# Expert layer 1's last table part in two classes, and the first group of the delta layer loaded, normalised and turned inside the expert layer's block

## The reference, cut to what matters

```python
x = x + linear_attention(layernorm(x))      # 16 heads, relu random features
x = x + expert_ffn(layernorm(x))            # 8 experts, top 2 of a softmax router
x = x + fast_weight_memory(layernorm(x))    # "delta": sequence over the 8 batches, own layer norm at its end
x = x + expert_ffn(layernorm(x))            # the same expert weights again
```

## Time and profile before

| what | value |
|---|---|
| median of 3 runs | 1044.81 us |
| the 3 runs | 1044.81, 1048.1, 1034.82 us |
| the profiled execution's own time | 1036.21 us |
| its span, first to last instruction | 1034.4 us |
| mean granted TensorE clock | 0.976 of full speed |
| PE busy | 946.9 us, 92% of the span |
| DVE, ACT, POOL busy | 54%, 52%, 36% of the span |

### The profile page before, as it was taken

How to read it: one execution, slowest core, us unless ns; L and a number is a source line. 1 busy time by engine, 2 the same in 40 slices (tenths; PEclk the granted TensorE clock), 3 DMA queues, 4 the chain that set the end, 5 groups by cost and what they waited for, 6 DMA issues and landing times.

```text
span 1034.4 us, 31649 instructions
## 1 busy us (share of the span) xinstructions
PE 946.9 (92%) x11919; PEld 701.9 (68%) x11919; DVE 553.6 (54%) x1979; ACT 534.6 (52%) x1082; POOL 367.6 (36%) x387
## 2 busy tenths in 40 slices
PE   7999999999999889969998899999999898897885
PEld 6445665566689889965544674595467697887775
DVE  5236355534574511207688478868768756671014
ACT  3443434342325344536776766775775754455553
POOL 2200331232135555543140102134321637465554
PEclk9999999999999899989999999999999999799998
DMA  8734412441213223213020301020216222223236
GB/s 219 209 83 83 105 48 63 98 104 47 66 51 86 66 69 83 59 58 125 4 83 18 83 29 34 13 92 19 60 51 220 60 57 66 55 58 85 76 110 205
DMA packets 80308, 82.77 MB, mean 80 GB/s; under 512 B 12207, under 2 KB 63236, under 8 KB 79648
## 3 DMA queue, kind: packets, MB, share of 16 engines
q1 hardware_dynamic: 66512, 59.87, 22.3%
q0 software_dynamic: 10176, 19.04, 6.0%
q10 hardware_dynamic: 3472, 1.84, 0.8%
HBM read 53.96 MB, written 27.64 MB: 79 GB/s over the span
## 4 chain that ended last, share of the span: by engine, by line
PE 37%; DVE 7%; ACT 5%; issue 3%; another core or an unknown queue 2%; DMA 1%; POOL 0%; ACTq 0%; POOLq 0%; DVEq 0%; SPq 0%
PE b_ring L1917 8%; PE b_ring L1366 6%; PE b_ring L1859 5%; PE b_ring L1377 5%; PE b_g L1970 4%; PE b_g L1939 4%; PE b_ring L1987 3%; DVE b_kq L2347 2%; ACT early L2102 2%; ACT b_v L1392 1%; ACT b_outT L2114 1%; ACT b_kq L1401 1%; PE b_r L248 1%; DVE b_coef L2258 1%
## 5 line engine op out<-in xcount | busy, mean ns | idle before, releaser
L1917 PE MATMUL b_ring<-b_hT,b_qkT 128*128 128x512 f32 x256 | 120.7, 608 | 5.3 <-DVE b_kq L2347 4.4
L2347 DVE SCALAR_TENSOR_TENSOR b_kq<-b_exp,b_ring 128x512 f32<-128x512 f32 x128 | 83.1, 684 | 35.6 <-ACT b_exp L2080 33.8
L1366 PE MATMUL b_ring<-b_v,b_kq 128*128 128x128 f32 x568 | 79.9, 285 | 23.9 <-ACT b_v L1387 20.2
L278 POOL DMA_INDIRECT expert_rows<-f_route_sent,f_route_place_id x64 | 62.0, 969 | 103.5 <-DVE f_route_place_id L234 50.8
L1366 PEld LDWEIGHTS b_ring<-b_v,b_kq 128*128 128x128 f32 x568 | 71.3, 197 | 30.9 <-ACT b_v L1387 25.8
L2080 ACT ACTIVATE b_exp<-b_ring 128x512 f32<-128x512 f32 x128 | 73.6, 604 | 29.7 <-PE b_ring L1917 17.5
L1366 PE MATMUL a_ring<-phik 128*128 128x128 f32 x568 | 78.8, 283 | 9.9 <-ACT phik L1387 9.2
L1917 PEld LDWEIGHTS b_ring<-b_hT,b_qkT 128*128 128x128 f32 x256 | 45.3, 189 | 61.4 <-issue 39.4
L278 POOL DMA_INDIRECT expert_rows<-g_route_sent,g_route_place_id x48 | 53.3, 1110 | 87.9 <-PE b_ring L1987 33.5
L1039 ACT ACTIVATE phik<-a_ring 128x512 f32<-128x512 f32 x64 | 38.2, 597 | 81.4 <-PE a_ring L882 79.1
L1366 PEld LDWEIGHTS a_ring<-phik 128*128 128x128 f32 x568 | 71.4, 197 | 12.6 <-ACT phik L1387 10.5
(11 more groups left out here) (344 smaller groups left out, 1854.6 us busy)
## 6 DMA issues: line engine op xcount, KB each, us to landing
a_rn_wide<-norm_compact SPq DMA_DIRECT2D x28, 512.0 KB, 10.0
wide<-in_L_ffn_W SPq DMA_DIRECT2D x32, 256.0 KB, 6.5
a_rn_wide<-expert_rows SPq DMA_DIRECT2D x71, 65.0 KB
b_coef<-gram_compact SPq DMA_DIRECT2D x4, 1024.0 KB, 4.9
b_hT<-expert_rows SPq DMA_DIRECT2D x56, 65.0 KB
x<-in_L_attn_a_x SPq DMA_DIRECT2D x8, 256.0 KB, 4.2
early<-expert_parts SPq DMA_DIRECT2D x4, 512.0 KB
gram_compact<-wide SPq DMA_DIRECT2D x32, 64.0 KB
```

The source lines that it names most:

```text
L278: pool.indirect_dma_start(self.rows, bass.IndirectOffsetOnAxis(self.place_id[:, k, n:n + 1], 0), self.sent[:, n, k, :], None).then_inc(sel ...
L1366: ins = pe.matmul(self.hid_bank[j % 2][:, f * P:(f + 1) * P], self.w1_now[:, b % W1_SLOTS, f * P:(f + 1) * P], self.blkT[:, b % HID_SLOTS, ...
L1917: pe.matmul(ring[n % 4][:, :], w, hT[:, g % 2, half * 512:half * 512 + 512], start=True, stop=True)\
L2347: dve.scalar_tensor_tensor(out=kq[:, p % 2, half:half + FOURS // 2, slot:slot + T * FOUR], in0=exps[:, n % EXPS, :].rearrange("p (a n) -> ...
```

## The change

1. The second table part is made in two classes of rows: first all rows that were routed up to the first of the last batch's four tiles, then the rest. `marked` is the router's count at that point. `A_NEXT` = 65: all rows of group 0 lie in blocks 0 to 64. The number of blocks stays 71.
2. SP loads group 0 when the blocks below `A_NEXT` are stored (with pairs, blocks 0 to 65), all four DMAs on SP, into `early`. It waits for the rest of the scatters behind the load. ACT loads nothing.
3. Five of the nine weight fills are turned beside blocks j = 22, 24, 26, 28 and 30, the other four behind the last block, in the two banks `a_y` and `a_t`.
4. DVE's additions, statistics and normalisation of group 0, POOL's roots, PE's turn and ACT's copy stand at the end of the first block (`FirstGroup`). The ones in `hT` are set by DVE at j = 30.
5. The block ends with `no_gpsimd_drain=True`.
6. `mix`, `own` and the router's start stand between the `kq` steps 15, 23 and 27 of group 0. SP loads groups 1, 2 and 3 without a wait.
7. `h` and `hT` and one buffer of the attention share a new tile `late`.

```diff
+A_NEXT = (2 * (TOKENS - (SEQ - P)) + EXPERTS * (P - 1)) // P
...
         block_table = BlockTable(K, C, "f", rows, rn_flat[...][:, 0:1280], ((0, A_FULL), (A_FULL, BLOCKS)),
+                                 {1: 1}, router.before[:, 1, :])
-        block = ctx.enter_context(nc.Block())
+        turn_banks, TURNED_BESIDE, TURN_AT = (y_bank, t_bank), 5, 22
+        block = ctx.enter_context(nc.Block(no_gpsimd_drain=True))
...
                 ffn.fetch(sp, j)
-            load_first_part(sp, K, C, ffn, parts, 0)
+            memory_weights.rows_turned(sp, K, TURNED_BESIDE)
+            ffn.stored_before(sp, A_NEXT)
+            first_group.load(sp)
+            ffn.stored(sp)
...
+                elif j in range(TURN_AT, TURN_AT + 2 * TURNED_BESIDE, 2):
+                    memory_weights.turn(pe, (j - TURN_AT) // 2, turn_banks)
+            for n in range(TURNED_BESIDE, memory_weights.FILLS):
+                memory_weights.turn(pe, n, turn_banks)
+            for half in range(2):
+                first_group.turn(pe, half, wide_bank[half])
...
-            load_first_part(act, K, C, ffn, parts, 1)
+                elif j in range(TURN_AT, TURN_AT + 2 * TURNED_BESIDE, 2):
+                    memory_weights.read(act, (j - TURN_AT) // 2, turn_banks)
+            for n in range(TURNED_BESIDE, memory_weights.FILLS):
+                memory_weights.read(act, n, turn_banks)
+            act.wait_ge(C["brows_less"], 15)
+            for half in range(2):
+                first_group.turned(act, half, wide_bank[half])
...
                 ffn.scatter(pool, j)
+            for half in range(2):
+                first_group.root(pool, half)
...
+                elif j == 30:
+                    first_group.ones(dve)
+            for half in range(2):
+                first_group.add(dve, half)
+            for half in range(2):
+                first_group.normalize(dve, half)
...
-            weights.turn(pe, weight_banks)
-            pe.wait_ge(weights.bank_read, weights.read0 + weights.FILLS)
-            turn(0)
             keys_and_queries(0)
...
+                    if g == 0 and n == 15:
+                        dve.memset(mix[:, :, :, :], 0.0)
+                    if g == 0 and n == 23:
+                        own_block()
+                    if g == 0 and n == 27:
+                        router.begin(dve)
```

More of the change, by code:

```diff
@@ L393, in count @@
             dve.tensor_copy(self.C["tail"][:, :], self.C["filled"][:, :]).then_inc(self.tail_ready, 1)
-        self.rows_of(dve, self.n_blocks, last)
-        if phase + 1 in self.marks:
+        if last and self.marked is not None:
+            self.rows_of(dve, self.touched[:, 0, :], True, self.marked)
+        self.rows_of(dve, self.n_blocks, last, self.C["filled"][:, :])
+        if phase + 1 in self.marks and self.marked is None:
             self.mark(dve, self.marks[phase + 1] - 1)
@@ L683, in less_last, with turn @@
         store_less_last(dve, C["beta_rows"][:, :, :], (C["brows_less"], 12), 0.0)
-    def turn(self, pe, banks):
+    def turn(self, pe, n, banks):
         C, ident = self.C, self.C["ident"]
[L690 to L703, removed]
@@ L721, in linear_attention @@
-def linear_attention(K, C, A, inp, normd, rows, parts):
+        b = banks[n % len(banks)]
+        if n >= len(banks):
+            pe.wait_ge(self.bank_read, self.read0 + n - len(banks) + 1)
+        if n < 6:
+            for j in range(4):
+                ins = pe.transpose(b[:, j * P:(j + 1) * P], C["b_rows"][:, 4 * n + j, :], ident[:, :])
+        elif n == 6:
+            ins = pe.transpose(b[:, 0:HEADS], C["beta_rows"][:, 0, :], ident[0:HEADS, 0:HEADS])
+        else:
+            for j in range(4):
+                q = 4 * (n - 7) + j
+                ins = pe.transpose(b[:, j * P:(j + 1) * P], C["wo_rows"][:, q * P:(q + 1) * P], ident[:, :])
@@ new lines, in turn, with read @@
+        ins.then_inc(self.bank_full, 1)
+    def read(self, act, n, banks):
+        C = self.C
+        b = banks[n % len(banks)]
+        act.wait_ge(self.bank_full, self.full0 + n + 1)
+        if n < 6:
+            dst, o = (C["b_qkT"], n) if n < 4 else (C["b_vT"], n - 4)
+            ins = act.copy(dst[:, o * 512:o * 512 + 512], b[:, :])
+        elif n == 6:
+            ins = act.copy(C["b_betaT"][:, 0:HEADS], b[:, 0:HEADS])
+        else:
+            ins = act.copy(C["b_oT"][:, 4 * (n - 7):4 * (n - 7) + 4, :], b[:, :].rearrange("p (a c) -> p a c", a=4))
+        ins.then_inc(self.bank_read, 1)
@@ new lines, in turn_half, with copy_turned @@
+def turn_half(pe, C, bank, h, slot, q):
+    for j in range(4):
+        ins = pe.transpose(bank[:, j * P:(j + 1) * P].rearrange("c (a j b) -> c j a b", j=2, b=T),
+                           h[:, slot, 4 * q + j, :], C["ident"][:, :])
+    return ins
+def copy_turned(act, hT, bank, slot, q):
+    return act.copy(hT[0:DIM - 1, slot, :].rearrange("c (a t b) -> c t a b", t=T, b=FOUR)[:, 4 * q:4 * q + 4, :, :],
+                    bank[0:DIM - 1, :].rearrange("c (t a b) -> c t a b", t=4, b=FOUR))
@@ L728, in linear_attention @@
         phik = K.sb(ctx, "phik", [P, NT, HD])
-        phiqT = [K.sb(ctx, f"phiqT{i}", [P, PAIRS, SEQ]) for i in range(2)]
+        phiqT = [K.sb(ctx, "phiqT0", [P, PAIRS, SEQ]), C["late"][:, :].rearrange("p (a n) -> p a n", a=PAIRS)]
         rn_wide = K.sb(ctx, "a_rn_wide", [P, PAIRS, SEQ])
@@ L2129, in take @@
                     ffn.take(act.copy, act, j)
-            weights.read(act, weight_banks)
-            act.wait_ge(C["brows_less"], 15)
-            turned(0)
             keys_and_queries(0)
```

129 lines of the change are left out of this document (62 added, 67 removed).

## The result

The changed kernel takes 1035.99 us (median of 20 runs, 1028.07 to 1042.06) against 1041.16 us for the kernel before (median of 20, 1034.82 to 1048.1). The ratio is 0.9948, with a 95% interval of 0.9928 to 0.9968. So it gains some 5 us (3.3 to 7.5 by the interval), real but well inside 2%. The forecast was 1037.1, within 2%. Two executions of one kernel can differ by 13 us, but 20 of each tell a change of 0.5% from none; the forecast's remark that under 2% nothing can be told was too cautious.

The account below looks back on a forecast made before the run. PE was taken to bound the expert layer's last blocks and the key stage, with a serial handover between them. From 1041.0 us, 5.9 gained there less 2.0 for the clock, net 3.9, gave 1037.1 us, range 1028 to 1047.

Parts of the forecast that it names:

- step 1: Expert layer 1, blocks 22 to 30: five weight fills moved there make everything behind come 2.3 us later, bounds 0 and 2.7.
- Step 2: Behind the last output product: the other four fills take some 3 us, to 462, and nothing waits for them.
- Step 3: Group 0's load: SP starts at 455.3, data takes 3.2 us (bounds 2.5 and 4.6), DVE starts at 458.5.
- rival D: Group 0's load lands late, 4.6 us instead of 3.2: gain 2.5, 1038.5 us; chance counted within the forecast's 0.53.
- Step 4: Group 0's chain, DVE's first addition to ACT's second copy: still 9.7 us, plus 0.3 for half-clock transposes, ending at 468.5.
- Step 5: First block's end without POOL's DRAIN: ACT's 0.15 plus 0.25 us to go on, at 468.9.
- Rival B: At the block's end, the jump to other code stalls 2.0 to 3.1 us: gain about 1, 1040 us; chance 0.17.
- The clock: Start of the key products: PE's silence leaves half clock for some 5 us, losing 2.0 us (1.0 to 2.6).
- Rival A: Between the stages, the clock holds and fills hide in PE's waits: gain up to 8.2, 1033 us; chance 0.15.
- What costs nothing: Added table steps (6.4 us on DVE), W1 and ACT copies, `ones`, `mix`, `own` and later loads fit into slack or pauses.
- POOL's DRAIN: First block's end: it takes 7.0 us, ending 5.1 us past the last scatter and last of all; the change removes it.
- Rival C: Expert layer 1 itself slows through PE stops, about 4.3 us each; from two on about 1046 us; chance 0.15.

Follow-up runs that it names:

- r2: The changed kernel again, unchanged, on a 975 us chip: 972.25 us, ratio 0.9963 to the kernel before.
- r1: The changed kernel, unchanged, timed again on the 1041 us chip: 1034.96 us, ratio 0.9945 to the kernel before.
- e4: The changed kernel with 40, 2 and 8 idle transposes where PE was silent: 968.64 against 975.22 us for the kernel before, ratio 0.9934.
- e8: The kernel before with only the second table part made in two classes: 976.80 against 974.54 us, ratio 1.0012.
- r3: The changed kernel with all nine fills behind the last block and 2 and 8 idle transposes, 975 us chip: 968.77 against 974.54 us before, ratio 0.9946.
- e1: The kernel before with only POOL's DRAIN at the first block's end left out: 978.65 against 975.22 us, ratio 1.0041.
- e7: The kernel before without that POOL DRAIN, plus 20 idle transposes behind the last weight fill: 975.27 against 974.54 us, ratio 1.0001.
- e2: The changed kernel with POOL's DRAIN kept at the first block's end: 975.51 against 975.22 us for the kernel before, ratio 1.0014.
- e5: The changed kernel with all nine weight fills behind the last block, group 0 in other tiles: 1029.36 us, ratio 0.9892 to the kernel before.
- r0: The kernel before, unchanged, traced again on the chip where it takes 1041 us.
- e6: The changed kernel with all nine fills behind the last block and 2 and 8 idle transposes, 1041 us chip: 1031.20 us, ratio 0.9909 to before.

## Why the prediction was right, point by point

The mechanism was as forecast: the load beside the last scatters, the chain ahead of the block's end, no DRAIN, and part of it given back by the clock. The net was forecast at 3.9 us, and the first sum products came 4.0 us earlier; the medians differ by 5.2. On a chip without stops the same sum is smaller: M falls by 3.9 (25.64 to 21.72), L grows by 2.5, so 1.4 are left. The terms below say why: 3.9 less 1.07 for the load and 0.56 for the clock is 2.3, and the first trace's 4.0 less 1.7 of luck (step 1) is 2.3 as well. So the sum of the trace was some 2 us too good. The whole times don't contradict it, for the ratio of r2 stands for a gain of 3.6 us, between 1.8 and 5.6; that this is more than the 1.4 of its trace, and the first 5.2 more than 2.3, no run explains.

- *Step 1, fills beside the blocks, 2.3 us.* Right where the layer has no stops: a block with a fill takes 2.33 us and one without 1.90, so 0.43 to 0.44 each and 2.2 for five, and L grew by 2.5. In the first trace it is buried: the weighing is only 0.56 later, for the stops of the two executions differ. So that trace's 6.6 us at the beta logits has some 1.7 of luck in it.
- *Step 2, the last four fills.* Right: done at 459.5, and nobody waits. They end 2.2 us behind the weighing's start where the forecast has 2.9, which makes PE's silence longer.
- *Step 3, the load.* SP issued it 3.85 us ahead of the last weighing, as the forecast has it (455.3 against 456.79 + 2.3). But from issue to DVE's addition it took 4.27 us, above the 3.2 taken and inside the bound of 4.6. So DVE starts 0.4 us behind the weighing where the forecast has it 0.6 ahead: the mis-sized term of this sum, some 1.0 us, and most of rival D. In the clock of the trace it doesn't show (457.8 against 458.5), for step 1's luck covers it.
- *Step 4, the chain of 9.7 + 0.3.* From the addition to the beta logits 10.43 us with the block's end, forecast 10.4. POOL's first root hid as forecast.
- *Step 5, the block's end, 0.4.* 0.36 us from ACT's last copy to PE. Rival B fell: no stop at the jump. (In its reading of the earlier trace rows PE stood until 384.82, 0.6 us longer than ACT.) By the Trainium skill (page "Runtime: NRT & Kernel Launch", section "Instruction fetch mechanics") a taken branch to a page outside the two that are held forces a DMA fetch. The changed kernel's trace shows none at the jump: from 455 to 470 us it has no packet of an instruction queue.
- *The clock, 2.0.* Measured 2.56 at the keys. It was half for 5.2 us behind the beta logits' start, at the upper end of the 1.0 to 2.6 given. In r1 it was 1.8 (9.43 against 7.63) and in r2 2.9 (10.52), past that end. Rival A's price for the clock was about right and its condition wrong: PE's silence is 5.3 us long, not 4, and the 3.2 us after which the clock fell before are no fixed time. In r2, the changed kernel again, it fell 1.4 us behind PE's last work. e4 shows that what A would have brought can be had: 2.2 to 3.7 us.
- *What costs nothing.* This step failed in one item. Of the W1 copies behind the table's steps it says that they "run five blocks ahead". e8 shows one that comes late and stops PE for 1.4 us. In the changed kernel (r2) no block there is longer than 2.33, for the fills have slowed PE at the same place, and the block that stopped in e8 takes 2.18: the two costs lie over each other. When r3 took the fills away, L fell by 1.1 only, not by 2.2, and that block took 3.3 us again.
- *POOL's DRAIN.* I took its end as tied to the last scatter and its removal as part of one sum. e1 and e7 show that alone it is worth nothing, and with the low clock less than nothing (+0.41%); e2 shows that it is tied to POOL's last instruction, and that the moved chain needs it gone: 2.0 to 2.4 us at the beta logits, 1.0 to 2.4 at the sums.
- *Rival C.* Where there are no stops, the layer is slower by step 1's 2.2 us and by 0.3 in the block that stopped in e8, and by nothing else.

## What to carry to other kernels

A handover between two stages has a length set by its first late input: move that first (here the load, 8 us), and the rest only pays behind it. Then look at what TensorE does in the silence that is left: work moved earlier can open a gap in front of the next TensorE-bound stage, and 50 useless transposes in it gave back 2.2 to 3.7 us of M, where the whole change had brought 3.9 to 5.4. Whatever fills such a gap should leave no pause in it (the clock fell in e5 and r3, where TensorE paused between the pieces), and it shouldn't reach past the next barrier (r3). Whether useful work is better placed there than in blocks where TensorE is already full isn't shown: e4 and r3 come out alike.

## What the runs showed of the hardware

- GpSimd's DRAIN at the end of a block that holds indirect DMAs took 6.1 to 7.0 us and ended 5.1 us behind GpSimd's last instruction, the scatter in one kernel, a 1.0 us arithmetic instruction in the other (e2), though there the last scatter had ended 4.8 us before that one.
- The time from TensorE's last work to the fall of the granted clock to 1.2 GHz wasn't the same from one execution to the next: 3.8, 2.2 and 1.4 us in three of the changed kernel (its first trace, r1, r2), 3.2 and 2.3 in two of the kernel before (its first trace, r0). In e5 it fell in a stretch in which TensorE still worked at intervals. With idle transposes in the gaps it held (e4, e6), and the same transposes failed to hold it in one execution on another chip (r3).
- The same kernel takes 975 us on two chips and 1041 on another. In a window of 130 us in the expert layer TensorE rests for 10 us there and for none here, in stops of ACT and DVE of up to 5.5 us (r0); the layer is 18 us longer. What causes them is open.
